# An AdaLN block on one core: pass B 12 quads behind pass A in place of 13, four hand-placed steps moved with it, and POOL's attention step put ahead of Q's split

## The reference, cut to what matters

```
h = _layernorm(x) * (1 + ca) + sa
Q = (h @ Wq.T).reshape(16, b, s, 8)            # K and V the same way
out = einsum(softmax(einsum(Q, K)), V).reshape(b, s, -1)
y = out + h
x = x + ga * (y - mean(y)) / sqrt(var(y) + EPS)     # mean and var over a whole batch
h = _layernorm(x) * (1 + cb) + sb
x = x + gb * experts(h)                             # top 2 of 8, H = 256
```

## Time and profile before

| | us |
|---|---|
| median of 3 runs | 1188.89 |
| lowest and highest of them | 1186.67, 1191.47 |
| the profiled execution | 1192.29 |
| its span | 1190.5 |
| stages 0 to 15, first to last maximum | 42.0 to 839.0 |
| last quad of pass B ends, blocks begin | about 877 |

### The profile page before, as it was taken

One profiled execution on the slowest core, in us unless ns is written; L12 is line 12 of the kernel. 1 busy time (PEld: TensorE's weight loads), 2 busy tenths in 40 slices (PEclk: granted clock), 3 DMA queues, 4 the chain that ended last, 5 costly groups with the idle time before them and its releaser, 6 DMA issues. The chain is left out here.

```text
span 1190.5 us, 19925 instructions
## 1 busy us (share of the span) xinstructions
PE 1027.4 (86%) x5891; PEld 391.0 (33%) x5891; DVE 926.0 (78%) x1972; ACT 845.1 (71%) x1597; POOL 695.2 (58%) x1094
## 2 busy tenths in 40 slices
PE   4699989899988989988888889889889999979970
PEld 2122222222222222222222222222247666656740
DVE  6799998988889898888989888999626565545873
ACT  2138887878787787878778786878876777746740
POOL 3833236465575756657475664553746667777771
PEclk9999998989898898989999998999899999989995
DMA  9879677464555746556584655521454232354985
GB/s 205 150 133 253 155 156 156 112 132 131 112 157 91 163 116 128 146 105 157 86 166 125 114 145 98 150 80 40 135 151 115 86 101 77 105 159 140 283 274 174
DMA packets 389884, 165.49 MB, mean 139 GB/s; under 512 B 291584, under 2 KB 359056, under 8 KB 385936
## 3 DMA queue, kind: packets, MB, share of 16 engines
q1 hardware_dynamic: 367312, 126.06, 47.7%
q0 software_dynamic: 9984, 20.60, 5.1%
q10 hardware_dynamic: 12480, 17.57, 4.1%
HBM read 91.84 MB, written 75.78 MB: 141 GB/s over the span
## 5 line engine op out<-in xcount | busy, mean ns | idle before, releaser
L1175 DVE TENSOR_REDUCE neg_max<-bank 128x1 f32<-128x512 f32 x1024 | 643.6, 680 | 75.5 <-PE bank L1865 74.3
L1642 ACT ACTIVATE probs<-bank 128x512 f32<-128x512 f32 x1024 | 547.6, 605 | 135.0 <-PE bank L1877 134.0
L1865 PE MATMUL bank<-Kt,Qt 48*128 48x512 bf16 x1024 | 356.4, 414 | 75.7 <-DVE neg_max L1175 67.3
L1877 PE MATMUL bank<-Qt,Kt 51*128 51x512 bf16 x1024 | 347.8, 404 | 16.8 <-ACT probs L1642 16.3
L1890 PE MATMUL bank<-probs,Vt 128*16 128x512 f32 x2048 | 286.1, 632 | 0.0
L1087 POOL DMA_INDIRECT y_dram<-y_rows,row_in x184 | 180.8, 982 | 71.0 <-issue 52.6
L1865 PEld LDWEIGHTS bank<-Kt,Qt 48*128 48x128 bf16 x1024 | 76.2, 95 | 434.0 <-DVE neg_max L1175 402.5
L1011 POOL DMA_INDIRECT rows_dram<-rows,slot x128 | 126.7, 990 | 46.9 <-issue 35.7
L1769 ACT ACTIVATE probs<-bank,w3b_cur 128x512 f32<-128x512 f32 x92 | 63.0, 687 | 71.7 <-PE bank L1959 71.7
L1528 DVE SCALAR_TENSOR_TENSOR probs<-bank,w3b_cur,probs 128x512 f32<-128x512 f32 x92 | 68.9, 749 | 41.1 <-ACT probs L1769 40.9
L1877 PEld LDWEIGHTS bank<-Qt,Kt 51*128 51x128 bf16 x1024 | 75.8, 94 | 58.8 <-ACT probs L1642 54.2
(11 more groups left out here) (208 smaller groups left out, 1263.6 us busy)
## 6 DMA issues: line engine op xcount, KB each, us to landing
o_dram<-o_sb ACTq DMA_DIRECT2D x64, 256.0 KB
row_in<-rows_dram SPq DMA_DIRECT2D x46, 260.0 KB, 2.8
Qt<-q_dram SPq DMA_DIRECT2D x64, 128.0 KB
Kt<-k_dram SPq DMA_DIRECT2D x64, 128.0 KB
y_in<-y_dram SPq DMA_DIRECT2D x16, 512.0 KB, 6.0
q_dram<-q_parts SPq DMA_DIRECT2D x48, 128.0 KB, 5.0
k_dram<-k_parts SPq DMA_DIRECT2D x48, 128.0 KB, 5.1
rows_dram<-rows SPq DMA_DIRECT2D x4, 1040.0 KB, 5.4
```

What stands on the lines that cost most here:

```text
L1175: dve.tensor_reduce(neg_max[:, side, a, col:col + 1], score_a[m % 3][:], AX_X, ALU.max, negate=True).then_inc(s_max, 1)
L1642: act.activation(probs[:, 4 * (j % 2) + (k ^ 1)], score_b[n % 3][:], ACT.Exp).then_inc(s_exp, 1)
L1865: pe.matmul(score_a[m % 3][:], Qt[b % BUFS][first:first + ROWS, n, P * c:P * c + P], Kt[b % BUFS][first:first + ROWS, n], start=True, stop ...
L1877: pe.matmul(score_b[m % 3][:], Kt[b % BUFS][first:first + ROWS + PARTS, n, P * c:P * c + P], Qt[b % BUFS][first:first + ROWS + PARTS, n], ...
```

## The change

Five edits. LAG goes from 13 to 12. Both turns of the maxima stand one quad sooner (2 to 1, and 10 to 9). x's transpose goes from quad 1 to quad 2. In POOL's list `add_h` stands ahead of `split_q`, and `x_rows` goes from in front of side 0's split to behind `y_move`, in front of `places`.

```diff
-LAG = 13
+LAG = 12
...
-        (2, "max_rows", b - 1, 1), (5, "h_turn", b - 3, 0), (7, "logits", b - 3, 0), (13, "pos", b - 3, 0), (8, "mean", b - 2, 0),
-        (10, "max_rows", b, 0), (11, "var", b - 2, 0), (15, "z_turn", b - 2, 0),
+        (1, "max_rows", b - 1, 1), (5, "h_turn", b - 3, 0), (7, "logits", b - 3, 0), (13, "pos", b - 3, 0), (8, "mean", b - 2, 0),
+        (9, "max_rows", b, 0), (11, "var", b - 2, 0), (15, "z_turn", b - 2, 0),
...
-    uses += [(q, what, b + 2, 0) for q, what in ((1, "x_turn"), (3, "q"), (4, "k"), (12, "v"))]
+    uses += [(q, what, b + 2, 0) for q, what in ((2, "x_turn"), (3, "q"), (4, "k"), (12, "v"))]
...
                 if has(b, 3, NB):
                     front_rows(b - 3)
-                if has(b, 1, NB - 3):
-                    split_q(b + 2)
                 if has(b, 2, NB + 1):
                     add_h(b - 2)
                 if has(b, 1, NB - 3):
+                    split_q(b + 2)
                     split_k(b + 2)
                 if b == 2:
                     idle_rows(3)
-                if has(b, 1, NB - 4):
-                    x_rows(b + 3)
...
                 if has(b, 2, NB - 1):
                     y_move(b - 2)
+                if has(b, 1, NB - 4):
+                    x_rows(b + 3)
                 if b == NB:
                     y_normal(b - 2)
```

## The result

| | before | after |
|---|---|---|
| median of 3 runs, us | 1188.89 | 1156.55 |
| lowest and highest | 1186.67, 1191.47 | 1153.14, 1157.02 |
| span of the profiled execution | 1190.5 | 1154.8 |

The ratio is 0.972, 95% interval 0.968 to 0.976. A second set of runs of the changed kernel, on another occasion, gave 1154.65. The change gains 32.3 us; 44.8 were forecast, so 12.5 are missing. The sign was right, and so was the mechanism in the main. The time lies inside the whole range (1134 to 1169), but not inside the forecast's own, 1134 to 1152. Of the missing time 3.4 us are no fault of a term: the terms were read from an execution 3.4 us above the median and taken off the median. Between the two profiled executions the gain is 35.7 us, and some 9 are missing.

A forecast was written before the change was run, and what follows sets the result against it. No engine was full; DVE's wait for `y` in stages 3 to 13 and TensorE's low clock behind it were taken to bound the kernel. 35.5 + 2.4 + 6.9 = 44.8 us off 1188.9 gave 1144.1 us, range 1134 to 1169 (own range 1134 to 1152).

The forecast's parts named there:

- Quads 6 to 9: Stages 3 to 13: DVE's wait for `y` (17.4 us) and what follows it, mostly low clock (18.1), go; 35.5 us.
- the comparison with stages 14 and 15: Priced quads 6 to 9 of stages 3 to 13 at those stages' 12.28 us each: 170.57 - 11 x 12.28 = 35.5.
- The cover of 2.2 us: POOL, stage 9: attention and h put first end at 506.54, DVE wants `y` at 508.73; 2.2 us in hand.
- the operands 3.7 us sooner: Attention's operands are ready 3.7 us sooner on POOL, 15.75 us after stage 9's start, as stage 14's 15.3 shows.
- x's rows behind `y_move`: POOL: some 2.2 us of work go into a 4.25 us gap where it waits for DVE's `pos`; nothing.
- Side 0's turn: Quad 9: split ready near 27.2 us, PE's slot near 26.7; taken at nothing, up to 0.5 us a stage.
- ACT's copy at quad 12: Copy of `o_sb` a quad sooner brings `z` 0.49 us sooner in stages 2 to 15; 6.9 us, bounds 0 and 10.2.
- Side 1's turn and quads 1 to 4: Turn in quad 1 has 1.3 us in hand; ACT paces quads 1 to 4, losing and gaining a copy; nothing.
- LAG's quad: Stage 16: pass B's last quad alone disappears, 2.06 us of exponentials and 0.37 of idle time; 2.4 us.
- The clock rival: PE's 1.20 us idle stretch at stage start still brings the clock down, 18.1 us not gained; 1162 us, chance 0.16.
- Late operands: Attention's operands aren't there at 503.8, `y` comes when it did, only 2.4 + 6.9 gained; 1179.6 us, chance 0.05.
- The slower rival: Side 1's turn in quad 1 becomes the bound when POOL's x's rows are held up; about 1196 us, chance 0.04.

The follow-up runs named there:

- the rest alone: Kernel before with only 12 quads and the turns in quads 1, 9 and 2, POOL's order as before; 1178.4 us, ratio 0.989.
- the later `tied`: Changed kernel with DVE's `tied` step three maxima later, in front of quad 9's first one; 1141.58 us, 0.9605 of the kernel before.
- x's rows in their old place: Changed kernel with x's rows back ahead of side 0's split; 1166.2 us, ratio 0.980.
- Q's split in front again: Changed kernel with Q's split in front of attention and h again on POOL; 1180.2 us, ratio 0.992.
- y's statistics three times: Changed kernel with DVE taking y's statistics two times more in quad 7 of stages 3 to 13; 1165.1 us, ratio 0.980.
- attention and h first: Kernel before with only attention and h put ahead of Q's split on POOL; 1181.2 us, ratio 0.993.
- statistics two tiles later: Kernel before with DVE taking y's statistics two maxima later, in the middle of quad 7, POOL's order untouched; 1176.7 us, ratio 0.990.
- POOL alone: Kernel before with only POOL's edits (attention and h first, x's rows behind `y_move`), 13 quads, turns as before; 1169.8 us, ratio 0.983.
- POOL alone and the later `tied`: Kernel before with all POOL edits, 13 quads, and `tied` moved to quad 9's start; 1156.6 us, ratio 0.972.
- the experiment with 13 quads: Changed kernel with only LAG put back to 13, turns and POOL's order left as changed; 1190.1 us, ratio 1.001.

## Why the prediction was right, and where its size was off

**Quads 6 to 9, 35.5 us forecast, 26.1 measured.** This is the mis-sized term. The mechanism (the wait goes, and with it the clock falls behind it) held in the changed kernel: `y_stats` waits for nothing in stages 3 to 13, and the clock is 1.00 in ten of the eleven. It held by the help of another part of the change, though, as the paragraph on x's rows says. The step that failed is the comparison with stages 14 and 15: "none of it lies in quads 6 to 9 except POOL's splits". I counted the splits as nothing, since POOL isn't waited for there. But they hold DVE: stages 14 and 15 have no K split for `tied` to meet. The difference, 11 x (13.13 - 12.28) = 9.4 us, is nearly what `tied` takes beyond its 0.22 us (0.93 in each of 11 stages, 10.2), and with `tied` moved the term is 36.1. The forecast's way of reading it was sound for all but the port.

**The cover of 2.2 us, the operands 3.7 us sooner.** Right: attention starts without idle time 15.6 us after the stage's start (486.59 - 470.97; I had said 15.75), and `y` is 2.1 us early.

**x's rows behind `y_move`, taken at nothing.** Right for the changed kernel as a cost, but the move isn't neutral. Put back, x's rows cost 9.6 us, through `y_dev` and through PE's wait for side 0's split; with 13 quads they cost 11.4. The prediction had the second in view only as an estimate of PE's slot in quad 9, and the first not at all. Since the 35.5 were read from stages without x's rows, this gain was in the term without a name. That was luck: in the prediction the move only serves side 0's split, and without it the falls that the 35.5 take as gone are still there in seven or eight stages (with 13 and with 12 quads).

**Side 0's turn, taken at nothing with up to 0.5 us a stage.** Right: PE's turn is done at 498.45 in stage 9, 27.5 us after its start, and doesn't wait.

**ACT's copy at quad 12, 6.9 us.** Right within its error: 6.2 us in stages 3 to 13, and 0.67 in stages 14 and 15 each, 7.5 together. It is 0.68 in a stage where I had 0.49, and the wait at quad 15 is down from 0.73 to 0.05 and not to 0.25. Stages 3 and 4 gain nothing there; ACT works on expert weights at that place.

**Side 1's turn and quads 1 to 4, taken at nothing.** A little was there: 1.9 us in stages 3 to 13, all in quad 3 (3.48 to 3.29), and 1.9 more in quad 3 of stages 14 and 15. Stages 0 to 2 lose 1.2; of these I can't name the cause.

**LAG's quad, 2.4 us.** In the profile only 0.9 remain, and the blocks take 1.9 us longer; the second profile of the changed kernel has stage 16 at 34.1, 2.2 us shorter than before. The kernels with 13 quads take 36.0 to 37.3 us for stage 16, all with a short fall of the clock in it; with 12 quads it is 31.5 where the clock stays up (the rest alone, the later `tied`) and 34.1 to 35.5 where it falls. So the edit can give 4.5 there. The prediction took stage 16 for its last quad alone and left out its clock, and that POOL and DVE's `w_parts` hold each other there, before and after.

**The rivals.** The clock rival fell: PE still idles 1.20 us beside `x_out` at the start of stage 9 (471.70), and the clock is 1.00 there, as it is behind this stretch in every stage from 3 to 13 of every profile. But its worry, that the clock falls for something else than `y`'s wait, came true in other kernels. PE's longest idle stretch in quads 6 to 9, and the stages of 3 to 13 with a fall behind it:

| kernel | longest idle stretch, us | stages with a fall |
|---|---|---|
| x's rows in their old place (stage 13 left out) | 1.67 | 8 of 10 |
| Q's split in front again; the rest alone | 1.65 | 10 of 11 each |
| before | 1.36 | 11 of 11 |
| y's statistics three times | 1.15 | 6 of 11 |
| attention and h first (stage 13: 0.47, and a fall) | 1.13 | 6 of 10 |
| statistics two tiles later (stage 13: 0.47, no fall) | 1.13 | 3 of 10 |
| POOL alone | 0.47 | 2 of 11 |
| the changed kernel, two profiles | 0.3 | 1 and 0 of 11 |
| POOL alone and the later `tied` | 0.34 | 0 of 11 |
| the changed kernel with the later `tied` | up to 0.3 | 0 of 11 |

The kernel with only LAG back at 13 has its three falls in quad 10, behind 0.54 us. So the falls get fewer as the stretch gets shorter, but its length doesn't decide: the same stretch brings a fall in one stage and none in the next, and the 1.20 us at the stages' start brings none. The rule of the Trainium skill cited in the prediction (TensorE: Matmul & The Clock Gate, "Why this matters for your kernels") blames gaps longer than any of these, so the traces speak against it as a full account. What decides is not settled by these runs. Late operands didn't occur. The slower rival's mechanism, side 1's turn as the bound, didn't either, but the experiment with 13 quads shows that quad 1 was the sensitive place: not POOL's slip, but ACT's copy and the issue of two DMAs there cost the whole gain.

## What to carry to other kernels

- When a comparison stage is used to price a change ("stage 14 has no wait"), list everything that it lacks, also on engines that nobody waits for: they can hold another engine without a semaphore. A small instruction whose time varies between 0.2 and 1.15 us in the same kernel, and always ends with one of POOL's, shows it.
- Once an engine runs ahead, its two-input steps on SBUF meet other work of POOL. Look at each of them in the new order, and move the cheap one: 13 us, 10 of them in stages 3 to 13, came with placing one 0.2 us step three tiles later.
- Positions that stand in one table (the lag of pass B and the quads of the turns) are one edit. Half of it took back all that the whole gained.

## What the runs showed of the hardware

- A step on 128 single numbers is held just as a larger one: `y_dev`, 0.16 us alone, takes 0.82 beside x's rows. In both sizes seen here (128x64 and 128x1) the price is the rest of POOL's instruction.
- It goes the other way too: beside DVE's two steps of `w_parts`, POOL's `y` took 3.20 us in place of 1.27, and the two steps took 5.49 us together in place of 4.54.
- A fall of the granted clock cost 0.4 to 3.0 us a stage, in stages with the same work (48.97 and 49.32; 48.58 and 50.20; 50.17 and 53.14). In stage 16, where PE sets the pace, 18 us at a mean of 0.53 made the stage 35.45 us long, where kernels with the same work and no fall took 31.5.
